# Layer 1 attention: the mask of each head moves from VectorE to GpSimd

## The chip, the cores and the metric

The kernel runs on one core of one Trainium2 chip. The metric is the device time of one launch in microseconds (us). The core has TensorE (PE) for matmuls, VectorE (DVE), ScalarE (ACT), GpSimd (POOL) and SyncE (SP), which issues the DMAs. Each engine works through its own instruction stream in order; between engines only semaphores order the work.

## The reference

Two transformer layers on 4 sequences of 1024 tokens with 128 channels. The change lies in the attention of layer 1, which keeps only the largest 30% of the scores of each row (`topk = 307` of 1024) and takes the softmax over those:

```python
topk = max(1, int(Tx * 0.3))
scores = jnp.einsum('bhid,bhjd->bhij', q, k) * scale
topk_scores, indices = jax.lax.top_k(scores, topk)
masked = jnp.full_like(scores, -jnp.inf)
masked = masked.at[bi, hi, ti, indices].set(topk_scores)
attn = jax.nn.softmax(masked, axis=-1)
out = jnp.einsum('bhij,bhjd->bhid', attn, v)
```

There are 16 heads and 32 blocks of 128 query rows, so 512 pairs of block and head, each with a score tile of 128 x 1024.

## The kernel before

`attention1` treats the 512 tiles ("heads" below) as a software pipeline written out by hand. Every engine runs the same frame, `tile_slots`: 16 slots for the first row block, a loop of 31 passes of 16 slots, and a tail. In slot h an engine does its own steps for heads h, h-1, h-2 and so on, by fixed lags. What a head goes through:

- TensorE, lag 0 (L1087): scores into the PSUM tile `S`. ScalarE (L1148) counts signs and makes a threshold `thr1` (L1159).
- VectorE, lag 1 (L1334): `z = S + thr1` into one of 8 ring buffers of `z`, with the row maximum. ScalarE (L1155) counts the signs of `z` and releases `cnt2`.
- GpSimd (its own slot h, after `cnt2` of head h): `shifted` (L1215), `side` (L1217), the large one `near` (L1221, 128 x 1024), and `rank` (L1224). In every fourth slot `split_max` (L1195 to L1205, five small steps for four heads) stands ahead of these, in another fourth slot `cut` and `gap` (L1229, L1232) stand behind them. `cut` is the exact threshold of each row for four heads.
- VectorE, lag 2: four MAX8 over quarters of `near` (L1363, L1373, L1379, L1391); lags 3 and 4: sorting the candidates, and `hits` (L1358), which finds the threshold `edge` and which reads two tiles in SBUF, `odd2` and `best`.
- VectorE, lag 8 (`PICK`): in every fourth slot the **check**: `flags` (L1325) from PSUM, and after `z` a load of its sum into a register (L1341) and a branch (L1342) that leads, for the rare rows with ties, into `general`, which rewrites `z` and `cut`. Then in every slot the **mask** (L1353): -2^40 where `z < cut`, into one of 4 buffers of `mask`.
- TensorE, lag 9: scores transposed plus mask, accumulated in `ST` (L1134, L1135); ScalarE takes the exponential (L1173); TensorE multiplies with v (L1103) four heads at a time.

In a VectorE slot the order is: (flags), wait for several semaphores, `z`, two small MAX8 (L1337, L1339), (register load, branch), wait `near_s` of head h-2, mask, `hits`, and the MAX8 mixed with the rest of the sort. The first wait for `near_s` stands ahead of the mask.

Of the kernel before, what the change touches and what calls it, by code (L numbers as in the profile page):

```python
# [930 lines left out]
def attention1(nc, k, search, ctx_all):  # L931
# [9 lines left out]
    with ExitStack() as ctx:  # L941
# [47 lines left out]
        mask_s, turned = sem("mask"), sem("turned")  # L989
# [193 lines left out]
        def _(pool):  # L1183
            CUTL = HIT - C2 - 1
# [22 lines left out]
            def slot(it, h):  # L1207
                n = lagged(it, h, 0, H, TOTAL)
                one = slice(h, h + 1)
                if n is not None:  # L1210
                    if h % 4 == 3:
                        pool.wait_ge(z_s, n + 1)
                        split_max(it, h)
# [10 lines left out]
                    pool.tensor_tensor(rank[:, one], sgn[1][:, one], shifted[:, one], ALU.mult).then_inc(rank_s, 1)  # L1224
                if lagged(it, h, CUTL, H, TOTAL) is not None and ends(h, CUTL):
                    l, h0 = nth(it, h, CUTL), (h - CUTL - 3) % H
                    four = slice(h0, h0 + 4)
                    pool.wait_ge(edge_s, l + 1)
                    pool.tensor_tensor(cut[:, four].bitcast(I32), side[:, four].bitcast(I32), edge[:, four].bitcast(I32),  # L1229
                                       ALU.subtract).then_inc(cut_s, 1)  # L1230

                    pool.tensor_tensor(gap[:, four], open_end[:, four], edge[:, four], ALU.subtract).then_inc(gap_s, 1)  # L1232
            tile_slots(pool, ITERS, H, CUTL + 1, slot)

        @block.vector
        def _(dve):
# [73 lines left out]
            def slot(it, h):  # L1310
# [38 lines left out]
                if picks:  # L1349
                    dve.wait_ge(cut_s, qp + 1)  # L1350
                    if not (isinstance(it, int) and lp < MASKS):
                        dve.wait_ge(turned, lp - (MASKS - 1))
                    dve.tensor_scalar(mask[:, hp % MASKS, :], z[:, hp % RING, :], cut[:, onep], AWAY,  # L1353
                                      ALU.is_lt, ALU.mult).then_inc(mask_s, 1)
# [662 lines left out]
```

## Time and profile before

| | us |
|---|---|
| median of 3 runs (4347.63 to 4366.65) | 4365.39 |
| the profiled execution | 4367.98 |
| its span, first to last instruction | 4366.2 |

| engine | busy us of the span | share |
|---|---|---|
| PE | 3242.5 | 74% |
| DVE | 3235.7 | 74% |
| ACT | 2490.3 | 57% |
| POOL | 1618.3 | 37% |

The page gives, for each engine, the busy time and the share of the span; then the span in 40 slices, where a digit is the busy share in tenths. The sparsified attention of layer 1 runs from about 1338 us to 3927 us. The timeline views give the start of each instruction and its duration in us, and in brackets how long its engine had sat idle before it and what released it. "issue" means that the engine waited for nothing that the profile shows. DVEq are instructions that VectorE's sequencer handles by itself (register loads, branches).

### The profile page before, as it was taken

Reading aid. Unit: us, or ns where it says so; the run is one execution under the profiler, and the core shown is the slowest. Engines: PE = TensorE matmul, PEld = TensorE weight load, DVE = VectorE, ACT = ScalarE, POOL = GpSimd, SP = SyncE. Lnnn points to the kernel's source line nnn. Section 1 sums busy time; section 2 is a strip of 40 time slices with the busy share of each in tenths; the row PEclk is TensorE's granted clock in tenths of the full one; section 3 lists DMA queues with packets and bytes.
Section 4 is the critical chain, followed back from the end, with each engine's and each line's share of the span. In section 5 each row is a group of like instructions: output and inputs, shape, how many; then the busy total and the mean of one; then the engine's idle time right before and its main releaser. Section 6 shows DMA issues by size and latency. Waiting matters only on the chain. (4 is left out here: it accounts for less than half of the span.)

```text
span 4366.2 us, 94950 instructions
## 1 busy us (share of the span) xinstructions
PE 3242.5 (74%) x25462; PEld 1877.8 (43%) x25510; DVE 3235.7 (74%) x12640; ACT 2490.3 (57%) x4604; POOL 1618.3 (37%) x3134
## 2 busy tenths in 40 slices
PE   3688888859375877766776776777775777775999
PEld 1233333446252444433443443444443444444565
DVE  6677777421647999977998996999987999994444
ACT  2255555523216777766776775777775777772222
POOL 3000000100024555544554554555554555553000
PEclk8699999969665555555555555555555555556999
DMA  3222222000012000001000001000001000000000
GB/s 104 36 37 28 33 30 32 2 14 24 22 60 35 6 5 4 6 9 25 4 6 4 4 10 27 4 6 4 4 12 25 4 6 4 5 2 25 5 7 7
DMA packets 130762, 74.95 MB, mean 17 GB/s; under 512 B 72791, under 2 KB 115559, under 8 KB 130455
## 3 DMA queue, kind: packets, MB, share of 16 engines
q1 hardware_dynamic: 130455, 72.22, 9.4%
q14 instruction: 281, 2.30, 0.2%
q8 instruction: 26, 0.43, 0.0%
HBM read 52.15 MB, written 19.14 MB: 16 GB/s over the span
## 5 line engine op out<-in xcount | busy, mean ns | idle before, releaser
L1134 PE MATMUL a_ST<-a_qs,a_ks 75*128 (+1 forms) x4096 | 880.6, 303 | 203.4 <-ACT a_eT L1173 145.5
L1221 POOL TENSOR_TENSOR a_near<-a_side,a_z 128x1024 int32<-128x1024 int32 x512 | 968.3, 1891 | 45.3 <-POOL a_side L1217 5.1
L1155 ACT ACTIVATE a_signs<-a_z,a_tiny 128x1024 bf16<-128x1024 f32 x512 | 588.1, 1149 | 608.4 <-DVE a_z L1334 608.4
L1135 PE MATMUL a_ST<-ident_b,a_mask 128*128 128x128 bf16 x4096 | 895.7, 306 | 0.0
L1334 DVE TENSOR_SCALAR_CACHE_REDUCE a_z<-a_S,a_thr 128x1024 f32<-128x1024 f32 x512 | 657.3, 1284 | 128.4 <-DVE a_cand L1391 60.4
L1134 PEld LDWEIGHTS a_ST<-a_qs,a_ks 75*128 75x128 bf16 x4096 | 570.6, 141 | 348.7 <-issue 341.3
L1087 PE MATMUL a_S<-a_ks,a_qs 72*128 72x512 bf16 x1024 | 505.3, 595 | 266.1 <-DVE a_z L1334 164.2
L1148 ACT ACTIVATE a_signs<-a_S,search 128x1024 bf16<-128x1024 f32 x512 | 564.0, 1102 | 75.0 <-PE a_S L1087 75.0
L1135 PEld LDWEIGHTS a_ST<-ident_b,a_mask 128*128 128x128 bf16 x4096 | 582.0, 142 | 0.1
L700 ACT ACTIVATE a_eT<-a_ST 128x512 f32<-128x512 f32 (+3 forms) x768 | 360.2, 490 | 378.8 <-PE a_ST L653 265.3
L1173 ACT ACTIVATE a_eT<-a_ST 128x1024 f32<-128x1024 f32 x512 | 512.8, 1002 | 34.4 <-PE a_ST L1135 34.3
L767 DVE TENSOR_REDUCE a_mx<-a_S 128x1 f32<-128x512 f32 (+3 forms) x768 | 388.8, 536 | 173.1 <-PE a_S L637 124.1
L1103 PE MATMUL a_O<-a_eT,a_v 128*9 128x128 f32 x8192 | 476.7, 392 | 26.7 <-DMA a_v<-v_ones 26.7
L1353 DVE TENSOR_SCALAR a_mask<-a_z,a_cut 128x1024 bf16<-128x1024 f32 x512 | 386.1, 754 | 50.6 <-DVE a_best L1339 9.6
L1103 PEld LDWEIGHTS a_O<-a_eT,a_v 128*9 128x9 f32 x8192 | 243.2, 118 | 375.0 <-issue 287.2
L637 PE MATMUL a_S<-a_ks,a_qs 72*128 (+4 forms) x768 | 274.4, 362 | 122.2 <-DMA a_ks<-k_parts 85.7
L1215 POOL TENSOR_TENSOR a_shifted<-a_sgn,a_miss 128x1 f32<-128x1 f32 x512 | 97.0, 189 | 592.7 <-ACT a_signs L1155 592.7
L718 POOL TENSOR_TENSOR ctxT<-a_num,a_rden 128x512 f32 (+1 forms) x32 | 40.6, 1269 | 616.6 <-DVE a_rden L799 616.6
L650 PE MATMUL a_ST<-a_qs,a_ks 128*128 (+4 forms) x720 | 240.4, 337 | 18.2 <-ACT a_eT L700 12.8
L1087 PEld LDWEIGHTS a_S<-a_ks,a_qs 72*128 (+1 forms) x1024 | 78.1, 116 | 369.2 <-issue 329.7
L1379 DVE MAX8 a_cand<-a_near 128x8 f32<-128x256 f32 x512 | 215.2, 420 | 0.0
L1363 DVE MAX8 a_cand<-a_near 128x8 f32<-128x256 f32 x512 | 214.1, 418 | 0.9 <-POOL a_near L1221 0.9
(327 smaller groups left out, 5641.5 us busy)
## 6 DMA issues: line engine op xcount, KB each, us to landing
a_ks<-k_parts SPq DMA_DIRECT2D x288, 64.0 KB
a_qs<-q_parts SPq DMA_DIRECT2D x144, 64.0 KB
a_qs<-q_parts SPq DMA_DIRECT2D x288, 32.0 KB
a_qs<-a_flip SPq DMA_DIRECT2D x512, 0.8 KB
q_parts<-p_qp SPq DMA_DIRECT2D x48, 128.0 KB, 1.7
k_parts<-p_kp SPq DMA_DIRECT2D x48, 128.0 KB, 1.8
f_w<-L_ffn_W SPq DMA_DIRECT2D x16, 256.0 KB, 2.6
v_ones<-p_vst SPq DMA_DIRECT2D x8, 288.0 KB, 2.4
```

The lines of the kernel that those rows point to most:

```text
L700: act.activation(eT[:, gi % 4, p % G, 0:hi - lo], ST[p % 2][:, 0:hi - lo], ACT.Exp, scale=SCALE0).then_inc(e_done, 1)
L767: dve.tensor_reduce(mx[:, lo // CW, j * IB + i:j * IB + i + 1], S[r % 3][:, 0:hi - lo], AX, ALU.max).then_inc(max_s, 1)
L1087: mm = pe.matmul(S[h % 2][:, lo:lo + CW], qa, ks[0:STACK, h * SEQ + lo:h * SEQ + lo + CW], start=True, stop=True)
L1103: mm = pe.matmul(O[32 * j:32 * j + HD + 1, :], v[:, kb, head], eT[:, h0 % RING + j, kb * P:(kb + 1) * P], start=(kb == 0), stop=(kb == IB ...
L1134: pe.matmul(ST[:, block_of], ks[:, hl * SEQ + kb * P:hl * SEQ + (kb + 1) * P], qa, start=True, stop=False)
L1135: mm = pe.matmul(ST[:, block_of], mask[:, hl % MASKS, block_of], k.ident_b[:, :], start=False, stop=True)
L1148: act.activation(signs[:, h % 2, :], S[h % 2][:, :], ACT.Sign, bias=first[:, bass.ds(n, 1)], accum_out=sgn[0][:, one]).then_inc(cnt1, 1)
L1155: act.activation(signs[:, 2, :], z[:, hl % RING, :], ACT.Sign, bias=tiny[:, :], accum_out=sgn[1][:, hl:hl + 1]).then_inc(cnt2, 1)
L1173: act.activation(eT[:, hl % RING, :], ST[:, :], ACT.Exp, scale=SCALE1).then_inc(e_done, 1)
L1221: pool.tensor_tensor(near[:, h % 2, :].bitcast(I32), side[:, one].bitcast(I32).broadcast_to([P, SEQ]), z[:, h % RING, :].bitcast(I32), ALU ...
L1334: dve.tensor_scalar(z[:, h1 % RING, :], S[h1 % 2][:, :], thr1[:, one1], None, ALU.add, ALU.max, accum_out=zmax[:, one1]).then_inc(z_s, 1)
L1353: dve.tensor_scalar(mask[:, hp % MASKS, :], z[:, hp % RING, :], cut[:, onep], AWAY, ALU.is_lt, ALU.mult).then_inc(mask_s, 1)
```

## The change

The mask of a head is no longer an instruction of VectorE but one of GpSimd, placed behind `near` and `rank` with a lag of 6 in GpSimd's own slots (`MASKL = PICK - C2 - 1`). VectorE tells with a new semaphore `check_s` when the check of four heads is done; GpSimd waits for it, and for a free mask buffer (`turned`), ahead of `shifted`, `side` and `near` of the same slot. `split_max` now stands ahead of that wait. VectorE gets a new wait ahead of `z`: the mask of the head that used this ring buffer before (`mask_s`). The tail of GpSimd's slots grows to 7.

```diff
             def slot(it, h):
                 n = lagged(it, h, 0, H, TOTAL)
                 one = slice(h, h + 1)
+                if n is not None and h % 4 == 3:
+                    pool.wait_ge(z_s, n + 1)
+                    split_max(it, h)
+                picks = lagged(it, h, MASKL, H, TOTAL) is not None
+                lp, hp = nth(it, h, MASKL), (h - MASKL) % H
+                if picks:
+                    pool.wait_ge(check_s, it * QD + (h - MASKL) // 4 + 1)
+                    if not (isinstance(it, int) and lp < MASKS):
+                        pool.wait_ge(turned, lp - (MASKS - 1))
                 if n is not None:
-                    if h % 4 == 3:
-                        pool.wait_ge(z_s, n + 1)
-                        split_max(it, h)
                     pool.wait_ge(cnt2, n + 1)
...
                     pool.wait_ge(shifted_s, n + 1)
                     pool.tensor_tensor(rank[:, one], sgn[1][:, one], shifted[:, one], ALU.mult).then_inc(rank_s, 1)
+                if picks:
+                    pool.tensor_scalar(mask[:, hp % MASKS, :], z[:, hp % RING, :], cut[:, hp:hp + 1], AWAY,
+                                       ALU.is_lt, ALU.mult).then_inc(mask_s, 1)
...
                 if has1 is not None:
+                    if not (isinstance(it, int) and l1 < RING):
+                        dve.wait_ge(mask_s, l1 - (RING - 1))
                     dve.wait_ge(thr1_s, l1 + 1)
...
                         with dve.Fori(0, 4) as j:
                             general(j, hp, qp)
+                    dve.nop().then_inc(check_s, 1)
...
-                if picks:
-                    dve.wait_ge(cut_s, qp + 1)
-                    if not (isinstance(it, int) and lp < MASKS):
-                        dve.wait_ge(turned, lp - (MASKS - 1))
-                    dve.tensor_scalar(mask[:, hp % MASKS, :], z[:, hp % RING, :], cut[:, onep], AWAY,
-                                      ALU.is_lt, ALU.mult).then_inc(mask_s, 1)
```

Where the instructions stand. GpSimd, at the turn from the fourth group's slot with `cut` to the next slot, before (the names are tiles, `a_shifted` is `shifted`; in brackets the semaphores waited for):

```order
L1224 TENSOR_TENSOR a_rank<-a_sgn,a_shifted 128x1 [waits a1_shifted]
L1229 TENSOR_TENSOR a_cut<-a_side,a_edge 128x4 [waits a1_edge]
L1232 TENSOR_TENSOR a_gap<-a_open_end,a_edge 128x4
L1215 TENSOR_TENSOR a_shifted<-a_sgn,a_miss 128x1 [waits a1_count2]
L1217 TENSOR_SCALAR a_side<-a_sgn 128x1
L1221 TENSOR_TENSOR a_near<-a_side,a_z 128x1024 [waits a1_top,a1_side]
L1224 TENSOR_TENSOR a_rank<-a_sgn,a_shifted 128x1 [waits a1_shifted]
L1195 TENSOR_TENSOR a_negmax<-a_thr,a_zmax 128x4 [waits a1_z]
```

The same place of GpSimd's stream in the changed kernel (its line numbers are 6 higher from `shifted` on):

```order
L1230 TENSOR_TENSOR a_rank<-a_sgn,a_shifted 128x1 [waits a1_shifted]
L1232 TENSOR_SCALAR a_mask<-a_z,a_cut 128x1024
L1238 TENSOR_TENSOR a_cut<-a_side,a_edge 128x4 [waits a1_edge]
L1241 TENSOR_TENSOR a_gap<-a_open_end,a_edge 128x4
L1221 TENSOR_TENSOR a_shifted<-a_sgn,a_miss 128x1 [waits a1_count2,a1_turned,a1_check]
L1223 TENSOR_SCALAR a_side<-a_sgn 128x1
L1227 TENSOR_TENSOR a_near<-a_side,a_z 128x1024 [waits a1_top,a1_side]
L1230 TENSOR_TENSOR a_rank<-a_sgn,a_shifted 128x1 [waits a1_shifted]
L1232 TENSOR_SCALAR a_mask<-a_z,a_cut 128x1024
L1195 TENSOR_TENSOR a_negmax<-a_thr,a_zmax 128x4 [waits a1_z]
```

A mask now stands in each slot, ahead of `cut` and ahead of `split_max` of the next slot, and `near` stands behind the wait for `check`.

VectorE, behind the branch of a check slot, before:

```order
L1352 REGISTER_ALU [waits a1_cut,a1_near,a1_sort]
L1353 TENSOR_SCALAR a_mask<-a_z,a_cut 128x1024 [waits a1_turned]
L1357 REGISTER_ALU [waits a1_rank]
L1358 SCALAR_TENSOR_TENSOR a_hits,a_edge<-a_odd,a_rank,a_best 128x24 [waits a1_sort]
L1361 MATCH_REPLACE a_rest<-a_best,a_cand 128x32
```

The same place in the changed kernel:

```order
L1363 REGISTER_ALU [waits a1_rank,a1_near,a1_sort]
L1364 SCALAR_TENSOR_TENSOR a_hits,a_edge<-a_odd,a_rank,a_best 128x24 [waits a1_sort]
L1367 MATCH_REPLACE a_rest<-a_best,a_cand 128x32
```

The mask is gone, and `hits` is the first instruction behind the wait for `near`.

## Rows read from the trace of the kernel before

**Rows 1.** The page: busy time and share by engine, and the 40 slices.
```profile
PE 3242.5 (74%) x25462; PEld 1877.8 (43%) x25510; DVE 3235.7 (74%) x12640; ACT 2490.3 (57%) x4604; POOL 1618.3 (37%) x3134
...
DVE  6677777421647999977998996999987999994444
```

**Rows 2.** Busy time by stretch: stage, one loop pass, one group of four slots.
```profile
core 0: us, PE busy (x) PEld busy (x) DVE busy (x) ACT busy (x) POOL busy (x), PEclk, DMA share, GB/s
2467.36:2545.47 78.11, 62.28 (x564) 37.43 (x564) 71.13 (x324) 58.55 (x108) 45.19 (x92) 0.52 0.03 5
...
2486.66:2505.75 19.09, 15.83 (x142) 9.40 (x143) 17.77 (x81) 14.64 (x28) 11.19 (x24) 0.50 0.00 1
1337.60:3926.80 2589.20, 1911.47 (x17729) 1153.88 (x17730) 2280.72 (x10355) 1863.76 (x3436) 1444.07 (x2940) 0.54 0.05 9
```

**Rows 3.** Timeline of VectorE: a check slot and the next `z`.
```profile
2505.75 1.28 DVE L1334 TENSOR_SCALAR_CACHE_REDUCE a_z<-a_S,a_thr 128x1024 f32<-128x1024 f32 x1 [0.26 <-DVE a_flags L1325]
...
2507.07 0.18 DVE L1339 MAX8 a_best<-a_cand 128x8 f32<-128x32 f32 x1
2507.28 0.75 DVE L1353 TENSOR_SCALAR a_mask<-a_z,a_cut 128x1024 bf16<-128x1024 f32 x1
2507.95 0.23 DVE L1358 SCALAR_TENSOR_TENSOR a_hits<-a_odd,a_rank,a_best 128x24 f32<-128x24 f32 x1
...
2510.39 1.28 DVE L1334 TENSOR_SCALAR_CACHE_REDUCE a_z<-a_S,a_thr 128x1024 f32<-128x1024 f32 x1 [0.24 <-DVE a_cand L1391]
```

**Rows 4.** VectorE's sequencer, 2440 to 2520 us: load of the flags' sum and branch.
```profile
L1342 DVEq COMPARE_BRANCH  x4: 56/70/72, 2447.1 to 2506.5; - x4
```

**Rows 5.** Timeline of GpSimd beside those slots.
```profile
2503.86 0.19 POOL L1215 TENSOR_TENSOR a_shifted<-a_sgn,a_miss 128x1 f32<-128x1 f32 x1
...
2504.31 1.89 POOL L1221 TENSOR_TENSOR a_near<-a_side,a_z 128x1024 int32<-128x1024 int32 x1
2506.16 0.19 POOL L1224 TENSOR_TENSOR a_rank<-a_sgn,a_shifted 128x1 f32<-128x1 f32 x1
2507.12 0.20 POOL L1195 TENSOR_TENSOR a_negmax<-a_thr,a_zmax 128x4 f32<-128x4 f32 x1 [0.77 <-DVE a_z L1334]
2507.40 0.68 POOL L67 TENSOR_TENSOR a_parts<-a_negmax,ones 128x4 bf16<-128x4 f32 x1
2508.16 0.20 POOL L1201 TENSOR_TENSOR a_left<-a_negmax,a_parts 128x4 f32<-128x4 f32 x1
2508.44 0.20 POOL L67 TENSOR_TENSOR a_parts<-a_left,ones 128x4 bf16<-128x4 f32 x1
```

**Rows 6.** Timelines of VectorE and GpSimd: `z` of a head, then its `shifted`.
```profile
2477.06 1.28 DVE L1334 TENSOR_SCALAR_CACHE_REDUCE a_z<-a_S,a_thr 128x1024 f32<-128x1024 f32 x1 [0.24 <-DVE a_cand L1391]
```
```profile
2479.71 0.19 POOL L1215 TENSOR_TENSOR a_shifted<-a_sgn,a_miss 128x1 f32<-128x1 f32 x1 [2.25 <-ACT a_signs L1155]
```

**Rows 7.** Groups of instructions by line: candidates for the mask's price on GpSimd.
```profile
L1353 DVE TENSOR_SCALAR a_mask<-a_z,a_cut 128x1024 bf16<-128x1024 f32 x512 | 386.1, 754 | 50.6 <-DVE a_best L1339 9.6 <-issue 6.4 <-DVE a_flags L1325 1.0
```
```profile
L1221 POOL TENSOR_TENSOR a_near<-a_side,a_z 128x1024 int32<-128x1024 int32 x512 | 968.3, 1891 | 45.3 <-POOL a_side L1217 5.1
...
L713 POOL COPY a_vx<-a_vst 128x128 f32 x28 | 8.2, 291 | 37.0 <-PE a_O L667 37.0
L882 POOL COPY o_c_in<-ctx 128x512 f32 x8 | 4.9, 612 | 19.8 <-PEq L889 19.0 <-PE o_cT_ps L897 0.8
```

**Rows 8.** Durations in ns (min/median/max): a VectorE op with two SBUF inputs; two of GpSimd.
```profile
L324 DVE TENSOR_TENSOR p_qres<-p_qf,p_qp x16: 674/681/1611, 47.1 to 1292.7; 128x512 f32<-128x512 f32 x16
```
```profile
L1358 DVE SCALAR_TENSOR_TENSOR a_hits<-a_odd,a_rank,a_best x512: 226/238/243, 1346.1 to 3933.0; 128x24 f32<-128x24 f32 x171
```
```profile
L67 POOL TENSOR_TENSOR a_parts<-a_negmax,ones x128: 198/202/690, 1346.3 to 3923.0; 128x4 bf16<-128x4 f32 x128
```

**Rows 9.** Timelines of both engines near 48 us: L328 has two SBUF inputs.
```profile
48.25 1.52 DVE L328 TENSOR_TENSOR p_qp<-p_qres,p_qp 128x512 bf16<-128x512 f32 x1
```
```profile
48.03 1.20 POOL L409 TENSOR_TENSOR p_kres<-p_kf,p_kp 128x512 f32<-128x512 f32 x1 [43.41 <-ACT p_kp L395]
```

**Rows 10.** Timelines at the loop's top: VectorE, and GpSimd's `shifted` and `near`.
```profile
2466.96 0.15 DVE L1325 TENSOR_SCALAR_CACHE_REDUCE a_flags<-a_OT 1x4 f32<-1x4 f32 x1 [2.07 <-issue]
```
```profile
2474.89 0.19 POOL L1215 TENSOR_TENSOR a_shifted<-a_sgn,a_miss 128x1 f32<-128x1 f32 x1 [1.96 <-ACT a_signs L1155]
...
2475.42 1.89 POOL L1221 TENSOR_TENSOR a_near<-a_side,a_z 128x1024 int32<-128x1024 int32 x1 [0.16 <-POOL a_side L1217]
```

More of the change, by code:

```diff
@@ L988, in attention1 @@
         flag_p, flag_v, gap_s = sem("flag_p"), sem("flag_v"), sem("gap")
-        mask_s, turned = sem("mask"), sem("turned")
+        mask_s, turned, check_s = sem("mask"), sem("turned"), sem("check")
         pv, oc, ot, rd, normed = sem("pv"), sem("o_copied"), sem("o_turned"), sem("rden"), sem("normed")
@@ L1183, in _ @@
         def _(pool):
-            CUTL = HIT - C2 - 1
+            CUTL, MASKL = HIT - C2 - 1, PICK - C2 - 1
             pool.memset(miss2[:, :], 2 * MISS).then_inc(pool_const, 1)
@@ L1232, in slot @@
                     pool.tensor_tensor(gap[:, four], open_end[:, four], edge[:, four], ALU.subtract).then_inc(gap_s, 1)
-            tile_slots(pool, ITERS, H, CUTL + 1, slot)
+            tile_slots(pool, ITERS, H, MASKL + 1, slot)
         @block.vector
```

## The prediction

> **What bounds the kernel now.** I read the page first: PE and DVE are both busy 74% of the span, but DVE's slices stand at 9 and above through most of the layer 1 attention [rows 1]. The busy time by stretch says what that stage is worth: 2589 us, and in a clean group of four slots DVE is busy 17.8 of 19.09 us, ACT 14.6, PE 15.8 and POOL 11.2 [rows 2]. So DVE's order of work sets the slot. Then the timelines. One loop pass of 16 heads takes 78.11 us [rows 2], of which 2.07 us are a stall of DVE at the loop's top [rows 10]; (78.11 - 2.07) / 4 = 19.0 us for a **group** of four slots. There are 128 groups.
>
> POOL looks half idle, but it isn't free at any time. It can begin `near` of a head only after that head's `z` on DVE and the sign count on ACT, and DVE wants `near` in its very next slot. The reader is to see in [rows 5] that `near` ends at 2506.20 and in [rows 3] that DVE passes its wait for it ahead of 2507.28: only 1.1 us of slack in each slot.
>
> **What is removed.** The mask on DVE: 754 ns [rows 7], start to start 0.67 us (2507.28 to 2507.95, [rows 3]), four per group: -2.68 us. If nothing else moved: 512 x 0.67 = 343 us. Also, `split_max` on POOL was stretched where it met the mask (0.68 against 0.20 us, [rows 5]); it now takes 4 x 0.28 + 0.15 = 1.27 us.
>
> **What is added on POOL: the mask's price M.** No row has a tensor-scalar of this size on POOL. From below: COPY, also one tensor input, 612 ns for 512 columns and 291 for 128 [rows 7], so 0.84 ns a column and 1.04 us for 1024. From above: `near`, two inputs, 1.89 us. It is nearer to COPY by its inputs, but it compares, multiplies and converts: I take M = 1.3.
> The Trainium skill (GPSIMD Engine Reference, Performance versus the Vector engine) gives 1.03 cycles an element at 1.2 GHz for bodies of at most two operations and 2.03 for comparisons that aren't unrolled: an estimate of 0.9 or 1.7 us, by which the sum below would be +0.1 or +1.3 us a group. Its advice (Engine selection) is to keep elementwise work on VectorE; the rows agree in so far as even COPY's rate is slower than the 0.75 us that DVE needs.
>
> **What is added as a wait.** `check_s` is raised by DVE in the check slot, and POOL waits for it ahead of `shifted`, `side`, `near` of the head whose `near` DVE wants in that same slot. Before, this `near` ran during the slot ahead. Queued behind the wait on POOL are `near`, `rank`, the mask, and the next slot's `split_max`; DVE waits for the first. How early is the check? The branch runs at 2506.5 [rows 4], 0.7 to 0.8 us after `z` began at 2505.75, so the sequencer runs ahead of DVE's own work; I put `check_s` at 0.85.
>
> **The group, step by step** (0 is the start of `z` in the check slot A; slots B, C, D follow). Constants: without the mask DVE is ready for `hits` 1.53 us after `z` starts (2505.75 to 2507.28); `hits` to the next `z` is 2.44 in A (2507.95 to 2510.39) [rows 3], which makes A 4.64 long; the other three slots share the remaining 14.36 of 19.0, 4.79 each, so 4.79 - 1.53 - 0.67 = 2.6 from `hits` to the next `z`. `shifted` to `near` 0.45, `near` 1.89 [rows 5]. `shifted` can't start before 2.65 after its head's `z` (2477.06 to 2479.71, [rows 6]), which puts `near`'s end 5.0 after `z`.
> - A: POOL starts at 0.9, `near` ends 3.25, DVE's `hits` 3.3 instead of 1.53: **1.75 us of stall**. Mask 3.35 to 4.65.
> - B: `z` 5.75, ready 7.3. POOL: `split_max` 1.27, `shifted`/`side` 0.45, `near` to 8.25. `hits` 8.3: **1.0 of stall**. Mask 8.35 to 9.65.
> - C: `z` 10.9, ready 12.45. `near` 10.1 to 12.0, mask 12.1 to 13.4.
> - D: `near` ends at 5.0 after C's `z`, 15.9; mask 16.0 to 17.3.
>
> In C and D `near` is in time, but DVE meets the mask itself. `hits` reads two SBUF tiles. The rows show such an instruction held while POOL works: L324 takes 674 or 1611 ns, never more in between than POOL's work explains, and L328 at 48.25 takes 1.52 us beside a POOL instruction that ends at 49.23 [rows 8, 9]; the other way round, `a_parts` is stretched to 690 by DVE's mask [rows 8]. So I let `hits` wait for the mask's end: C 13.4 instead of 12.45, **0.95 of stall**; D's `z` 16.0, ready 17.55, behind the mask's end, no stall; the next A's `z` at 17.55 + 2.6 = 20.15.
> The Trainium skill (SBUF — State Buffer, Who interferes with whom) states it as a lock: a VectorE instruction with two SBUF inputs and a GpSimd instruction that reads SBUF exclude each other for the whole instruction. L328's row agrees; for `hits`, never above 243 ns in 512 [rows 8], the trace before can't tell, since no long POOL instruction ran beside it.
>
> Sum: 20.15 - 19.0 = +1.15 us a group, x 128 = **+147 us**. The same steps with M = 1.04 give 19.4 (+0.4, 51 us), with M = 1.89 give 21.0 (+2.0, 256 us; there `near` is late in every slot, and `cut`, `gap` behind the last mask make the flags late).
>
> **The loop's top.** DVE stalls 2.07 us there for nothing shown; POOL sat idle 1.96 us at its own top and was still 0.16 late for `near` [rows 10]. So a reload of up to about 2 us is hidden under POOL's idle time now. Behind the change POOL has no idle time there (C follows a mask). Bounds 0 and 2.07 us x 31 = 64; I take 1 us: **+31**.
>
> **Hidden.** The new wait on `mask_s` ahead of `z` asks for a mask made 3 slots before its `z`: free up to M of 2.3 us. PE gets a mask up to 1.5 us later in the group; its transposed matmuls also wait for the exponential, which comes 2.6 us after `z` and later than the mask: 0. ACT is busy 14.6 of 19 [rows 2]: 0. The wait on `turned` is met by a slot: 0. `check_s` itself is a sequencer's step: 0.
>
> Forecast: span 4366.2 + 147 + 31 = 4544; the profiled run lies 1.8 us above its span and 2.6 above the median: **4543 us**.
>
> **Rivals.**
> 1. *`hits` loses the race* (0.2). When `near` ends, POOL goes on to `rank` and the mask 0.1 us later, and DVE's `hits`, released by the same event, comes while `rank` reads. If the mask gets in first, `hits` waits M more in A, and in B to the end of that mask. With M = 1.3: `hits` stands at 4.65, 9.65, 13.8 and 18.65, the next `z` at 21.25: +2.25 a group, with the loop's top 4366 + 288 + 31 = 4685. For: POOL's instructions start back to back [rows 5]. Against: DVE asks first.
> 2. *M near 1.9* (0.2): 4366 + 256 + 31 = 4653.
> 3. *M near COPY's* (0.2): 4366 + 51 + 31 = 4448, or 4417 without the loop term.
> 4. *No contention for `hits`* (0.1), if tiles of 24 columns don't hold DVE. Then only the stalls of A and B are left, 1.75 and M - 0.3, against 2.68 of masks: M = 1.3 gives `hits` at 3.3, 8.3, 12.45, 16.6 and `z` at 19.2 (+0.2, 26 us), M = 1.04 gives 18.95 (-0.05). With the loop's top between 4360 and 4423: mostly no change. **Faster** is this case with a cheap mask: it decides where M falls below 1.1; at VectorE's own 0.75 us the group is 18.65, -0.35, -45 us, 4321 without the loop term.
> 5. *The move acts as meant* (0.02): if `near` weren't behind the check, -343 us, 4023. The order rows speak against it.
>
> **How the numbers follow.** My own case has 0.28. The range holds it, rival 3, most of rivals 1 and 2 and the upper part of 4: 4385 to 4730; left out are M and a lost race together above, and a cheap mask below. Anything within 0.5% (22 us) is about what a measurement of this kernel can't tell from no change. Faster by more: 0.06 (rival 5 and the cheap end of 4). Within: 0.10 (most of the rest of 4, the low end of 3). Slower: 0.84.
>
> **What would show it.** In the changed profile: (a) the mask on POOL with its mean duration; (b) DVE idle ahead of `hits`, released by POOL's `near`, once or twice a group, some 1.8 and 1.0 us, in all above 300 us; (c) `hits` with a maximum far above 243 ns, or late by the mask's length, if contention is real; (d) POOL's busy time up by 512 x M; (e) a group of about 20.2 us and DVE's busy time down by 386 us; (f) an idle time of POOL at the loop's top. Wrong would be: `near` released ahead of the check, or M above 2.3, where the ring wait ahead of `z` bites.

## The result, and the profile after

The changed kernel takes **5494.01 us** in the median of 4 runs (5481.41 to 5500.54) against 4363.31 us (4347.63 to 4366.65) of the kernel before: ratio **1.2605**, 95% interval 1.2575 to 1.2634. It is slower, as forecast, but by 1131 us where 178 were forecast (4543, range 4385 to 4730).

The page of the changed kernel: busy time by engine, and the slices of VectorE and GpSimd. They answer to [rows 1].

```profile
PE 3262.7 (59%) x25510; PEld 1914.4 (35%) x25510; DVE 3304.4 (60%) x12128; ACT 2505.3 (46%) x4604; POOL 3461.2 (63%) x3646
...
DVE  5877762164666666666666666666666666664444
...
POOL 2000001013888987889798888889888988898200
```

GpSimd's busy time more than doubled (1618 to 3461 us), and in the attention stage its slices now stand at 8 and 9 where VectorE's have fallen to 6. The bound moved from VectorE to GpSimd. The stage by the busy times of a stretch, beside [rows 2]:

```profile
core 0: us, PE busy (x) PEld busy (x) DVE busy (x) ACT busy (x) POOL busy (x), PEclk, DMA share, GB/s
1357.90:5072.60 3714.70, 1925.82 (x17910) 1197.93 (x17910) 2337.05 (x9790) 1865.88 (x3408) 3265.58 (x3422) 0.53 0.03 5
```

GpSimd is busy 3266 of 3715 us. TensorE's granted clock is 0.53 in this stage, as before (0.54), so the clock isn't the cause. The groups of instructions by line say which instruction it is (columns: busy us, mean ns of one | idle time of the engine just before, with what ended it); the first two answer to [rows 7], the third to [rows 8]:

```profile
L1232 POOL TENSOR_SCALAR a_mask<-a_z,a_cut 128x1024 bf16<-128x1024 f32 x512 | 1908.4, 3728 | 2.0 <-DVEq L1356 2.0
L1227 POOL TENSOR_TENSOR a_near<-a_side,a_z 128x1024 int32<-128x1024 int32 x512 | 968.9, 1892 | 45.0 <-POOL a_side L1223 5.1
...
L1345 DVE TENSOR_SCALAR_CACHE_REDUCE a_z<-a_S,a_thr 128x1024 f32<-128x1024 f32 x512 | 657.4, 1284 | 355.5 <-POOL a_mask L1232 309.7 <-DVE a_flags L1334 30.9 <-ACT a_thr L1159 14.3
...
L1364 DVE SCALAR_TENSOR_TENSOR a_hits<-a_odd,a_rank,a_best 128x24 f32<-128x24 f32 x512 | 523.0, 1021 | 779.7 <-issue 324.9 <-DVE a_best L1350 202.2 <-POOL a_rank L1230 169.6
```

One mask costs GpSimd **3.73 us**, five times VectorE's 0.75 and twice `near`, which the prediction took for the upper bound. The timeline of GpSimd over a group (start us, duration; in brackets how long it was idle, and what released it), beside [rows 5]:

```profile
3002.23 3.73 POOL L1232 TENSOR_SCALAR a_mask<-a_z,a_cut 128x1024 bf16<-128x1024 f32 x1
3005.92 0.20 POOL L1238 TENSOR_TENSOR a_cut<-a_side,a_edge 128x4 int32<-128x4 int32 x1
3006.07 0.20 POOL L1241 TENSOR_TENSOR a_gap<-a_open_end,a_edge 128x4 f32<-128x4 f32 x1
3008.76 0.19 POOL L1221 TENSOR_TENSOR a_shifted<-a_sgn,a_miss 128x1 f32<-128x1 f32 x1 [2.48 <-DVEq L1356]
3008.91 0.23 POOL L1223 TENSOR_SCALAR a_side<-a_sgn 128x1 f32<-128x1 f32 x1
3009.22 1.89 POOL L1227 TENSOR_TENSOR a_near<-a_side,a_z 128x1024 int32<-128x1024 int32 x1
3011.07 0.19 POOL L1230 TENSOR_TENSOR a_rank<-a_sgn,a_shifted 128x1 f32<-128x1 f32 x1
3011.24 3.73 POOL L1232 TENSOR_SCALAR a_mask<-a_z,a_cut 128x1024 bf16<-128x1024 f32 x1
3014.93 0.20 POOL L1195 TENSOR_TENSOR a_negmax<-a_thr,a_zmax 128x4 f32<-128x4 f32 x1
...
3016.20 0.19 POOL L1221 TENSOR_TENSOR a_shifted<-a_sgn,a_miss 128x1 f32<-128x1 f32 x1
...
3022.38 0.19 POOL L1221 TENSOR_TENSOR a_shifted<-a_sgn,a_miss 128x1 f32<-128x1 f32 x1
```

A slot of GpSimd is 6.18 us (3016.20 to 3022.38) with nothing idle in it. A group is 4 x 6.18 = 24.7, plus 1.27 of `split_max` (3014.93 to 3016.20), 0.3 of `cut` and `gap`, and 2.48 idle at the wait for the check: 28.8 us. VectorE's `z` in the check slots stands 28.81 us apart (3007.21 and 3036.02), where it was 19.0 before. The stage has 29.0 us for each group (3714.7 / 128), so nearly all of it is this one chain. The same group on VectorE, beside [rows 3]:

```profile
3006.85 0.15 DVE L1334 TENSOR_SCALAR_CACHE_REDUCE a_flags<-a_OT 1x4 f32<-1x4 f32 x1 [1.50 <-PE a_OT L1113]
...
3007.21 1.28 DVE L1345 TENSOR_SCALAR_CACHE_REDUCE a_z<-a_S,a_thr 128x1024 f32<-128x1024 f32 x1 [0.21 <-DVE a_flags L1334]
...
3011.30 1.09 DVE L1364 SCALAR_TENSOR_TENSOR a_hits<-a_odd,a_rank,a_best 128x24 f32<-128x24 f32 x1 [2.60 <-POOL a_rank L1230]
...
3015.19 1.28 DVE L1345 TENSOR_SCALAR_CACHE_REDUCE a_z<-a_S,a_thr 128x1024 f32<-128x1024 f32 x1 [0.83 <-POOL a_mask L1232]
...
3018.74 1.10 DVE L1364 SCALAR_TENSOR_TENSOR a_hits<-a_odd,a_rank,a_best 128x24 f32<-128x24 f32 x1 [2.06 <-issue]
```

VectorE waits in each slot: ahead of `flags` (which need `gap`, and `gap` stands behind the fourth mask on GpSimd), ahead of `hits`, and ahead of `z` for a ring buffer that the mask still reads. And `hits`, 0.24 us of work, takes 1.1: it starts 0.06 us behind the mask.

### The profile page after: what moved, and what is told of

It reads as the page before. It is cut to its first block and busy times, and to the rows that moved or that the text cites. A ratio compares the mean times of both kernels' runs of the same rounds, so it can differ in the third digit from the quotient of the medians.

```text
span 5498.8 us, 95725 instructions
## 1 busy us (share of the span) xinstructions
PE 3262.7 (59%) x25510; PEld 1914.4 (35%) x25510; DVE 3304.4 (60%) x12128; ACT 2505.3 (46%) x4604; POOL 3461.2 (63%) x3646
## 5 line engine op out<-in xcount | busy, mean ns | idle before, releaser
L1232 POOL TENSOR_SCALAR a_mask<-a_z,a_cut 128x1024 bf16<-128x1024 f32 x512 | 1908.4, 3728 | 2.0 <-DVEq L1356 2.0
L1364 DVE SCALAR_TENSOR_TENSOR a_hits<-a_odd,a_rank,a_best 128x24 f32<-128x24 f32 x512 | 523.0, 1021 | 779.7 <-issue 324.9
L1345 DVE TENSOR_SCALAR_CACHE_REDUCE a_z<-a_S,a_thr 128x1024 f32<-128x1024 f32 x512 | 657.4, 1284 | 355.5 <-POOL a_mask L1232 309.7
L1087 PE MATMUL a_S<-a_ks,a_qs 72*128 72x512 bf16 x1024 | 538.7, 629 | 102.7 <-DMA a_ks<-k_parts 55.3
L1103 PE MATMUL a_O<-a_eT,a_v 128*9 128x128 f32 x8192 | 502.4, 409 | 32.7 <-DMA a_v<-v_ones 32.7
L409 POOL TENSOR_TENSOR p_kres<-p_kf,p_kp 128x512 f32<-128x512 f32 x16 | 21.6, 1350 | 399.9 <-ACT p_kp L395 399.9
L650 PE MATMUL a_ST<-a_qs,a_ks 128*128 (+4 forms) x768 | 259.9, 342 | 18.7 <-ACT a_eT L700 12.9
L1112 PE MATMUL a_OT<-a_twice,ones 128*1 128x4 f32 x256 | 24.8, 167 | 340.4 <-ACT a_hidden L1167 340.2
```

Source lines behind the costliest of these rows:

```text
L1087: mm = pe.matmul(S[h % 2][:, lo:lo + CW], qa, ks[0:STACK, h * SEQ + lo:h * SEQ + lo + CW], start=True, stop=True)
L1103: mm = pe.matmul(O[32 * j:32 * j + HD + 1, :], v[:, kb, head], eT[:, h0 % RING + j, kb * P:(kb + 1) * P], start=(kb == 0), stop=(kb == IB ...
L1232: pool.tensor_scalar(mask[:, hp % MASKS, :], z[:, hp % RING, :], cut[:, hp:hp + 1], AWAY, ALU.is_lt, ALU.mult).then_inc(mask_s, 1)
L1364: dve.scalar_tensor_tensor(hits[:, :], odd2[:, :], rank[:, one4], best[:, h4 % 2, :], ALU.is_equal, ALU.mult, accum_out=edge[:, one4]).the ...
```

## The experiments

First theory: the time is two costs that hardly overlap, the price of the mask on GpSimd and the wait for the check ahead of `near`. Rivals: the mask is slow only because VectorE is in its way; the wait costs nothing beside such a mask; a hold between the two engines makes the most of it.

**The price by itself.** The kernel before, with a tail on GpSimd behind its attention of layer 1: twelve forms of instruction, three times each, with no other work on GpSimd. Four of the first list:

```diff
+                pool.tensor_scalar(pb[:, :], px[:, :], pc[:, 0:1], AWAY, ALU.is_lt, ALU.mult).then_inc(price_s, 1)
...
+                pool.tensor_scalar(py[:, :], px[:, :], pc[:, 0:1], None, ALU.is_lt).then_inc(price_s, 1)
...
+                pool.tensor_scalar(py[:, :], px[:, :], 0.5, 2.0, ALU.mult, ALU.add).then_inc(price_s, 1)
...
+                pool.tensor_copy(py[:, :], px[:, :]).then_inc(price_s, 1)
```

> Price list: the kernel before, with a tail on GpSimd behind its slots of the layer 1 attention in which each of 12 forms of a 128 x 1024 instruction runs alone, three times, each behind the end of the one ahead. The mask's form (f32 in, a threshold for each row, is_lt then mult, bf16 out) took 3.73 us in the changed kernel. Theory 'form': it is the price of the two-step tensor-scalar itself, so it costs 3.7 us here too, with VectorE idle, 1.9 us at 512 columns, and about half with one step (is_lt alone). Rival 'contention': 3.73 us holds waits for VectorE, and alone it costs 1.0 to 1.9 us. Second rival 'output type': f32 out is clearly cheaper than bf16 out. COPY of 1024 columns should be 1.04 us by the two COPY rows of before.

One instruction's durations in ns (min/median/max) with their starts; L1241 is the mask's own form, L1245 the same into f32, L1249 the comparison alone, L1253 a multiplication alone, L1255 multiply and add, L1263 a copy:

```profile
L1241 POOL TENSOR_SCALAR a_pb<-a_px,a_pc x3: 3714/3714/4619, 3930.4 to 3990.3; 128x1024 bf16<-128x1024 f32 x3
L1245 POOL TENSOR_SCALAR a_py<-a_px,a_pc x3: 3703/3704/3704, 3937.3 to 3996.2; 128x1024 f32<-128x1024 f32 x3
L1249 POOL TENSOR_SCALAR a_py<-a_px,a_pc x3: 2843/2843/2844, 3944.0 to 4002.9; 128x1024 f32<-128x1024 f32 x3
L1253 POOL TENSOR_SCALAR a_py<-a_px x3: 2782/2782/2782, 3950.7 to 4009.6; 128x1024 f32<-128x1024 f32 x3
L1255 POOL TENSOR_SCALAR a_py<-a_px x3: 1047/1047/1048, 3953.5 to 4012.4; 128x1024 f32<-128x1024 f32 x3
L1263 POOL COPY a_py<-a_px x3: 1037/1042/1042, 3959.7 to 4018.6; 128x1024 f32<-128x1024 f32 x3
```

3.71 us in a quiet place: the price is the form's own, not VectorE's doing and not the conversion's (3.70 into f32). The 4.62 us is the first of the three; it ran beside the last four masks of VectorE. One step alone was expected at about half and takes three quarters (2.84). The copy at 1.04 us is what [rows 7] were read to give, but it says nothing about a comparison. A second list asked which forms are cheap.

> Second price list, as the first, with 12 other forms on GpSimd (128 x 1024 unless said). In the first list a tensor-scalar with two immediate steps mult, add took 1.05 us, one step is_lt 2.85, is_lt and mult 3.7, mult alone 2.78, and a tensor-tensor mult 1.89. Theory 'a fast path': only mult then add (perhaps also add or mult with a value for each row) is fast, about 1.05 us, and everything else costs 2.8 us for one step and 3.7 for two. Rival 'comparisons are slow': add, min and mult forms of any kind are at 1.0 to 1.9 us and only is_lt costs more. At 256 columns the mask's form should take 1.1 us (2.00 at 512 and 3.71 at 1024 make 3.35 ns a column and 0.28 us fixed).

```profile
L1243 POOL TENSOR_SCALAR a_py<-a_px,a_pc x3: 1117/1117/1423, 3925.6 to 3976.1; 128x1024 f32<-128x1024 f32 x3
L1245 POOL TENSOR_SCALAR a_py<-a_px,a_pc x3: 2850/2852/3196, 3927.1 to 3977.3; 128x1024 f32<-128x1024 f32 x3
L1253 POOL TENSOR_SCALAR a_py<-a_px x3: 3639/3639/3639, 3935.5 to 3985.4; 128x1024 f32<-128x1024 f32 x3
L1255 POOL TENSOR_SCALAR a_pb<-a_px,a_pc x3: 1189/1189/1189, 3939.3 to 3989.1; 128x1024 bf16<-128x1024 f32 x3
```

Add then multiply is 1.12 us (L1243), the add alone 2.85 (L1245), minimum then multiply 3.64 (L1253), multiply then add with two column operands 1.19 (L1255). One step is dearer than two: only the pairs of add and multiply that were tried are quick.

**The wait alone.** The mask stays on VectorE; only `check_s` is added, ahead of `shifted`:

```diff
+                    if lagged(it, h, PICK - C2 - 1, H, TOTAL) is not None:
+                        pool.wait_ge(check_s, it * QD + (h - (PICK - C2 - 1)) // 4 + 1)
                     pool.wait_ge(cnt2, n + 1)
...
+                    dve.nop().then_inc(check_s, 1)
```

> The kernel before, mask still on VectorE, with only the new wait: GpSimd waits for the check of four heads ahead of shifted, side and near. Theory 'price of the mask': the wait costs what step A of the prediction said, near ends 3.25 us after z of the check slot, VectorE ready at 1.53: +1.75 us a group, 224 us, about 4590 us; less if near stands nearer. Rival 'the wait is the cause': most of the +1130 us, above 5000 us. Rival 'hidden': no change.

Measured 4637.1 us, +274, ratio 1.0617 (1.0552 to 1.0683). A check slot, VectorE and then GpSimd:

```profile
3018.40 1.28 DVE L1336 TENSOR_SCALAR_CACHE_REDUCE a_z<-a_S,a_thr 128x1024 f32<-128x1024 f32 x1 [0.26 <-DVE a_flags L1327]
...
3021.97 0.75 DVE L1356 TENSOR_SCALAR a_mask<-a_z,a_cut 128x1024 bf16<-128x1024 f32 x1 [2.08 <-issue]
```
```profile
3019.54 0.19 POOL L1217 TENSOR_TENSOR a_shifted<-a_sgn,a_miss 128x1 f32<-128x1 f32 x1 [2.97 <-DVEq L1347]
...
3019.99 1.89 POOL L1223 TENSOR_TENSOR a_near<-a_side,a_z 128x1024 int32<-128x1024 int32 x1
```

VectorE comes to its next instruction 3.57 us after `z` began instead of 1.53 [rows 3]: 2.04 us a group, x 128 = 261 of the 274. GpSimd starts 1.14 us after `z` here; the prediction had 0.9.

**The mask alone.** The change with its two waits, for the check and for a free mask buffer, moved behind `near`:

```diff
-                if picks:
-                    pool.wait_ge(check_s, it * QD + (h - MASKL) // 4 + 1)
...
                 if n is not None:
                     pool.wait_ge(cnt2, n + 1)
...
+                if picks:
+                    pool.wait_ge(check_s, it * QD + (h - MASKL) // 4 + 1)
...
+                if n is not None:
                     pool.wait_ge(shifted_s, n + 1)
                     pool.tensor_tensor(rank[:, one], sgn[1][:, one], shifted[:, one], ALU.mult).then_inc(rank_s, 1)
```

> The changed kernel with the waits for the check and for a free mask buffer moved behind near, ahead of rank. The mask stays on GpSimd. Theory 'price': GpSimd is then never idle for long; its own work is 4 x (0.45 + 1.89 + 0.15 + 3.7) + 1.3 + 0.3 = 26.4 us a group against the 28.8 measured in the trace of the changed kernel: about -2.4 x 128 = -300 us, 5190 us. Rival 'the wait is the cause': back to within 250 us of before, 4400 to 4600 us.

Measured 5199.65 us, +836, ratio 1.1905 (1.1832 to 1.1978). GpSimd runs without a gap but for 1.6 us at the loop's top; a group is 26.46 us, 2.35 less than with the wait ahead. The two parts add up: 274 + 836 = 1110 of the 1131 us.

**A smaller price.** Both of the change's parts, but the mask covers only the first columns, 320 and 512 of 1024; the rest of `mask` stays zero, so part of the scores isn't masked.

```diff
-                    pool.tensor_scalar(mask[:, hp % MASKS, :], z[:, hp % RING, :], cut[:, hp:hp + 1], AWAY,
+                    pool.tensor_scalar(mask[:, hp % MASKS, 0:320], z[:, hp % RING, 0:320], cut[:, hp:hp + 1], AWAY,
                                        ALU.is_lt, ALU.mult).then_inc(mask_s, 1)
```

> The changed kernel, its mask made for the first 320 of 1024 columns alone (the rest of the mask stays zero, so the softmax runs over more scores than it should). If the price goes with the columns, the mask takes about 1.3 us, the value that the prediction took. Theory 'only M was wrong': the group is then 20.15 us by the prediction's steps and the time about 4543 us (4500 to 4600). Rival 'the steps are wrong too': outside 4450 to 4650 us.

> The changed kernel with the mask made for 512 of 1024 columns (the rest stays zero). Mask 2.0 us. By the prediction's steps the value for 1.89 us was 21.0 us a group, 4653 us; for 2.0 us about 21.5 a group, 4720 us. For hits, which lasted 1.10 us beside a mask of 1024 columns and 0.51 beside one of 320: theory 'it is held while GpSimd reads its input, 0.83 ns a column': 0.24 + 0.43 = 0.67 us. Rival 'it is held for the whole instruction': above 1.5 us.

Measured: 320 columns, mask 1.38 us, 4545.9 us, ratio 1.0408 (1.0348 to 1.0469); 512 columns, mask 2.02 us, 4724.1 us, ratio 1.0852 (1.0802 to 1.0902). With nearly the price that the prediction assumed (1.3), the time is nearly the one predicted (4543). Slots B and C of the first show that this is partly luck. GpSimd's masks of B and C, then VectorE's `hits` of B and C:

```profile
3014.70 1.38 POOL L1233 TENSOR_SCALAR a_mask<-a_z,a_cut 128x320 bf16<-128x320 f32 x1
...
3018.52 1.38 POOL L1233 TENSOR_SCALAR a_mask<-a_z,a_cut 128x320 bf16<-128x320 f32 x1
```
```profile
3014.75 0.51 DVE L1365 SCALAR_TENSOR_TENSOR a_hits<-a_odd,a_rank,a_best 128x24 f32<-128x24 f32 x1 [0.80 <-DVE a_best L1351]
...
3019.25 0.24 DVE L1365 SCALAR_TENSOR_TENSOR a_hits<-a_odd,a_rank,a_best 128x24 f32<-128x24 f32 x1
```

In B `hits` starts 0.05 us behind the mask and is held to 0.51; in C it starts in the middle of a mask that runs to 3019.90 and isn't held. So C's stall of 0.95 us doesn't exist, while A was worse than said: its `hits` began at 4.06 us after `z`, not 3.3, and was held 0.3 more, as it was in B. These errors nearly cancel: a group is 20.39 us where 20.15 was said. A held `hits` takes 0.51 us beside 320 columns (the row above), up to 0.67 beside 512 and 1.10 beside 1024: 0.24 us and 0.83 to 0.84 ns for each column of the mask, not the 3.35 ns a column that the mask's own duration has. The hold has a fixed end: in the changed kernel a `hits` that started 0.34 us into the mask instead of 0.05 took 0.81 us instead of 1.10, and both end 1.15 us after the mask's start.

**Both parts made small.** 320 columns (again part of the scores isn't masked) and the wait behind `near`.

> The changed kernel with both: the mask for 320 of 1024 columns (1.38 us, the rest zero) and the waits for check and mask buffer behind near instead of ahead of it. Theory 'two causes, each enough': with neither of them GpSimd's own work is 4 x (0.45 + 1.89 + 0.15 + 1.38) + 1.6 = 17.1 us a group, VectorE's is 16.3, so the group is 17.1 to 18.3 us against 19.0 before: faster, 4120 to 4280 us. Rival 'contention eats it': hits held twice or more a group, 19 us or above, 4360 us or more.

Measured 4230.83 us, ratio 0.9719 (0.9668 to 0.977). With a short mask and the wait out of the way, giving VectorE's mask away does gain. The question is then whether a complete kernel can get there.

**Sharing.** The kernel before, but GpSimd makes 448 columns of the masks of two heads in four, VectorE the rest; waits behind `near`.

```diff
+                if picks:
+                    pool.tensor_scalar(mask[:, hp % MASKS, 0:LEAD], z[:, hp % RING, 0:LEAD], cut[:, hp:hp + 1], AWAY,
+                                       ALU.is_lt, ALU.mult).then_inc(part_m, 1)
...
-                    dve.tensor_scalar(mask[:, hp % MASKS, :], z[:, hp % RING, :], cut[:, onep], AWAY,
+                    lo = LEAD if hp % 4 in SHARE else 0
+                    dve.tensor_scalar(mask[:, hp % MASKS, lo:], z[:, hp % RING, lo:], cut[:, onep], AWAY,
```

> An attempt at a better kernel, complete: the kernel before, in which GpSimd makes the first 448 of 1024 columns of the masks of the third and fourth head of each four (1.78 us each, in its idle time behind near) and VectorE the other 576 and the first two heads whole. VectorE saves 448 x 0.65 ns = 0.29 us twice a group, at most 128 x 0.58 = 75 us: 4290 us. Rival 'the shared port': VectorE's mask is held while GpSimd's part runs, or GpSimd's part while VectorE's runs, and near comes later: 4360 us or more.

Measured 4396.63 us, ratio 1.01 (1.0069 to 1.0131). A pair of the two parts, VectorE's and GpSimd's:

```profile
3010.89 0.79 DVE L1373 TENSOR_SCALAR a_mask<-a_z,a_cut 128x576 bf16<-128x576 f32 x1
```
```profile
3009.55 1.81 POOL L1238 TENSOR_SCALAR a_mask<-a_z,a_cut 128x448 bf16<-128x448 f32 x1
```

VectorE's 576 columns take 0.50 us at the shortest, but 0.67 in the mean of 256. When they started 1.25 to 1.5 us into GpSimd's part, as above, they took 0.62 to 0.87 us. When they started 0.97 to 1.16 us into it (98 of 256), they took 0.52, and GpSimd's part was stretched from 1.81 to 1.9 or 2.1. So VectorE saves 256 x (0.755 - 0.674) = 21 us of the 75 hoped for, and the kernel is 43 us slower; where those are lost wasn't looked for.

**Another form of the mask.** GpSimd computes the difference, VectorE turns its sign into the mask in place (bf16):

```diff
+                    pool.tensor_scalar(mask[:, hp % MASKS, :], z[:, hp % RING, :], cut[:, hp:hp + 1], 2.0 ** 60,
+                                       ALU.subtract, ALU.mult).then_inc(diff_s, 1)
...
+                if picks:
+                    dve.wait_ge(diff_s, lp + 1)
+                    dve.tensor_scalar(mask[:, hp % MASKS, :], mask[:, hp % MASKS, :], 0.0, AWAY, ALU.is_lt, ALU.mult).then_inc(mask_s, 1)
                 if has2 is not None:
                     dve.max(found[:, 24:32], quarter(3)).then_inc(top_s, 1)
```

> A complete kernel. GpSimd keeps the subtraction, VectorE keeps the comparison. The wait for the check stands behind `near` (as in e2_wait_behind). GpSimd writes (z - cut) * 2^60 into the mask's bf16 buffer: a two-step subtract-and-multiply, of the kind that the price runs show at 1.12 us instead of 3.73. VectorE turns it into the mask in place (is it below 0, times -1e30; bf16 in and out, no wait in the hot spot ahead of `hits`), just ahead of its last MAX8. The wait ahead of `z` for a free buffer goes by GpSimd's pass. My theory (two causes: the price of the form, and the wait that stands ahead of `near`; with both gone VectorE's work sets the group again): GpSimd per group 4 x (2.49 + 1.12) + 1.57 = 16.0 us, below VectorE's 16.3 + 4 x 0.35 = 17.7; a group of about 17.9 to 18.6 and a time of 4240 to 4330 us, faster than before. Rival (contention: `hits` is held while GpSimd reads, up to 0.85 us in two slots of four, and the small work behind the pass comes late): no gain, 4360 us or more.

> A complete kernel. The same two passes as f6_diff, but the wait for the check stands where the change put it, ahead of `shifted` and `near`. It is the change at the price of the mask that the prediction assumed (1.1 against 1.3 us), over all 1024 columns. With 320 columns and a mask of 1.38 us a group took 20.39 us; here GpSimd's pass is 0.26 shorter, VectorE has 0.35 more in each of four slots: between 20.1 (its added work falls into slots where it waited anyhow) and 21.8: 4460 to 4680 us, most likely 4580, slower than before. Rival (the wait matters only beside a long mask): about the time of f6_diff.

Both miss their ranges: 5496.17 us, ratio 1.2622 (1.2594 to 1.2649), and, with the wait ahead of `near`, 5788.02 us, 1.3283 (1.3246 to 1.3321). Subtract-and-multiply isn't one of the quick pairs:

```profile
L1233 POOL TENSOR_SCALAR a_mask<-a_z,a_cut 128x1024 bf16<-128x1024 f32 x512 | 1926.5, 3763 | 52.7 <-DVEq L1357 1.7
...
L1399 DVE TENSOR_SCALAR a_mask<-a_mask 128x1024 bf16<-128x1024 bf16 x512 | 218.6, 427 | 960.6 <-POOL a_mask L1233 960.6
```

I had inferred the price of `subtract` from that of `add` (1.12 us); it is 3.76. The price isn't all: with the same price and the same place of the wait e2_wait_behind took 5200 us. The other 297 us came with VectorE's second pass and its wait for GpSimd's (960.6 us in all); no run separates the two. So the next pair takes the measured form itself, z times -1 plus `cut`, and asks whether that is above 0:

```diff
-                    pool.tensor_scalar(mask[:, hp % MASKS, :], z[:, hp % RING, :], cut[:, hp:hp + 1], 2.0 ** 60,
-                                       ALU.subtract, ALU.mult).then_inc(diff_s, 1)
+                    pool.tensor_scalar(mask[:, hp % MASKS, :], z[:, hp % RING, :], less1[:, :], cut[:, hp:hp + 1],
+                                       ALU.mult, ALU.add).then_inc(diff_s, 1)
```

> A complete kernel: f6_diff with another form of the same pass. In f6_diff GpSimd's subtract-and-multiply took 3.76 us, the slow price. Here GpSimd computes cut - z as z times -1 (a column) plus cut (a column), the form that the second price run shows at 1.19 us, and VectorE asks whether that is above 0 (0.43 us, as measured in f6_diff). The wait stands behind `near`. By the rows of f6_diff GpSimd's four slots would take (7.96 - 3.77 + 1.19) + 2 x (6.69 - 3.77 + 1.19) + (6.98 - 3.77 + 1.19) = 18.0 us, VectorE's work is 16.3 + 4 x 0.43 = 18.0: both near the 19.0 of before. My theory (the price of the form is what cost f6_diff and the change their time): 1150 us or so below f6_diff, a group of 18.2 to 19.2 us, 4270 to 4400 us. Rival (VectorE's wait for GpSimd's pass, 960 us in f6_diff, is a matter of order and stays in part even with a short pass): above 4450 us.

> A complete kernel: f9_negdiff with the wait for the check where the change put it, ahead of `shifted` and `near`. It is the change with a short GpSimd pass (1.19 us; the prediction assumed 1.3) over all columns. The wait alone cost 2.1 us a group in e1_wait_alone. Theory (the wait costs that much whatever the mask): f9_negdiff + 128 x 2.1 = 270 us, between 4500 and 4680. Rival (the wait hides behind VectorE's wait for the pass): within 80 us of f9_negdiff.

The pass on GpSimd took 1.20 us as expected, but the kernel 4768.52 us, ratio 1.0939 (1.0917 to 1.0962). That is 728 us less than with the slow form, but neither the 4270 to 4400 of the theory nor the rival's reason: VectorE's wait for the pass has gone (5.0 us in all). A third cause is in the rows of VectorE's own pass over the mask; the line of durations, then VectorE and GpSimd in three slots:

```profile
L1399 DVE TENSOR_SCALAR a_mask<-a_mask x512: 396/1779/1946, 1360.7 to 4348.8; 128x1024 bf16<-128x1024 bf16 x171
```
```profile
3002.87 0.83 DVE L1365 SCALAR_TENSOR_TENSOR a_hits<-a_odd,a_rank,a_best 128x24 f32<-128x24 f32 x1
...
3005.26 0.40 DVE L1399 TENSOR_SCALAR a_mask<-a_mask 128x1024 bf16<-128x1024 bf16 x1
...
3015.72 1.78 DVE L1399 TENSOR_SCALAR a_mask<-a_mask 128x1024 bf16<-128x1024 bf16 x1
```
```profile
3002.47 1.20 POOL L1233 TENSOR_SCALAR a_mask<-a_z,a_less,a_cut 128x1024 bf16<-128x1024 f32 x1
...
3005.34 2.07 POOL L1223 TENSOR_TENSOR a_near<-a_side,a_z 128x1024 int32<-128x1024 int32 x1
...
3015.33 1.89 POOL L1223 TENSOR_TENSOR a_near<-a_side,a_z 128x1024 int32<-128x1024 int32 x1
```

Started 0.39 us behind `near`, VectorE's pass takes 1.78 us and ends 0.3 us after it (3017.50 against 3017.22); started 0.08 us ahead, it takes 0.40, and `near` is the one stretched, to 2.07. The mean is 1.37 instead of 0.43: 512 x 0.94 = 480 us of VectorE. `hits` is held too: started 0.40 us into GpSimd's pass, it takes 0.83 us and ends 0.03 us after it. With the wait put back ahead of `near` (f10_negdiff_wait) it is 4911.82 us, ratio 1.1272 (1.1243 to 1.1301), +143 where I had +270 or under 80. The pass meets `near` less often there (mean 1.10 us, 134 us less in sum) and `hits` is held less (57 us less), which pays for part of the wait.

Was it the hold? The same kernel with VectorE's pass moved up to between GpSimd's pass and the next `near`:

```diff
                     dve.match_replace(rest[0][:, :], ranked[:, 0:8], mine, GONE).then_inc(sort_s, 1)
+                if picks:
+                    dve.wait_ge(diff_s, lp + 1)
+                    dve.tensor_scalar(mask[:, hp % MASKS, :], mask[:, hp % MASKS, :], 0.0, AWAY, ALU.is_gt, ALU.mult).then_inc(mask_s, 1)
...
-                if picks:
-                    dve.wait_ge(diff_s, lp + 1)
-                    dve.tensor_scalar(mask[:, hp % MASKS, :], mask[:, hp % MASKS, :], 0.0, AWAY, ALU.is_gt, ALU.mult).then_inc(mask_s, 1)
```

> A complete kernel: f9_negdiff with VectorE's pass over the mask moved up, from behind the third MAX8 (where its trace shows it beside GpSimd's `near`, 1.78 us in the median instead of 0.43) to right behind `hits`' MATCH_REPLACE8, which by that trace lies between the end of GpSimd's pass and the start of the next `near`. Theory (a bf16 pass of VectorE and `near` keep each other out of SBUF, and that, 512 x (1.37 - 0.43) = 480 us, is why f9_negdiff is slower than before): the pass takes 0.4 to 0.6 us in the mean, VectorE waits for GpSimd's pass up to 0.6 us a slot instead; a group of 18.5 to 20 us, 4300 to 4480 us. Rival (the pass is slow for another reason, in place for instance, or `near` catches it here too): mean above 1.2 us and a time within 80 us of f9_negdiff's 4769.

```profile
L1371 DVE TENSOR_SCALAR a_mask<-a_mask x512: 408/416/478, 1357.2 to 3988.8; 128x1024 bf16<-128x1024 bf16 x171
...
L1365 DVE SCALAR_TENSOR_TENSOR a_hits<-a_odd,a_rank,a_best x512: 242/244/850, 1340.4 to 3980.4; 128x24 f32<-128x24 f32 x171
```

4423.19 us, 345 less by the place of one instruction, ratio 1.0146 (1.0129 to 1.0163) to the kernel before. The hold was the third cause. The move took 486 us from VectorE's pass (699 to 213 us in all); `hits` (34 us more) and new waits take part of that back. What is left over the kernel before is small change: 0.42 us of pass in each slot, `hits` held in some slots (mean 0.42 instead of 0.24), 62 us of waiting for GpSimd's pass. No complete kernel of these beats the one before.

## Why the prediction was wrong

- **The price M: the step that failed.** "It is nearer to COPY by its inputs [...] I take M = 1.3", between 1.04 and 1.89. The mask measured 3.73 us in place and 3.71 alone. Neither bound was one: no row of the trace before had a compare-and-multiply of any large size on GpSimd, and the number of inputs, by which I placed it, isn't what sets the price there. With a bound that doesn't exclude anything the range should have been open above. The Trainium skill (GPSIMD Engine Reference) has 1.03 cycles an element in the section Performance versus the Vector engine, and 2.03 for a comparison that isn't unrolled in the section Performance pitfalls for Q7 kernels; at its 1.2 GHz that is an estimate of 0.9 or 1.7 us. The measured 3.73 us is over twice the dearer one, so the trace disagrees. Only the add-and-multiply pairs, at 1.04 to 1.19 us, come near its cheap figure.
- **M above 2.3 and the ring wait.** The text named this as what would make it wrong, and it happened: VectorE waits 309.7 us ahead of `z` for GpSimd's mask. In those slots GpSimd has no idle time, so the wait is the form in which its pace reaches VectorE rather than a cost of its own.
- **"DVE's order of work sets the slot".** True before; behind the change GpSimd's 26.3 us of work a group (4 x 6.18 and 1.6) are above VectorE's 19.0 - 2.68 = 16.3. I added M to a chain of events slot by slot and never held GpSimd's sum against the group. With M = 1.3 that sum was harmless: the same slots would be 26.3 - 4 x 2.43 = 16.6 us.
- **The wait ahead of `near`.** Right in kind: slot A stalls, and e1_wait_alone has 2.04 us a group for it. The start of GpSimd in A was 0.9 in the prediction, 1.14 with the mask on VectorE and 1.55 in the changed kernel (3007.21 to 3008.76).
- **Who waits for whom at the check.** I priced the wait from VectorE's side only. It also closes a circle: `flags` need `gap`, `gap` stands behind the fourth mask on GpSimd, and GpSimd then waits for the check of those flags with nothing to do, 2.48 us a group, x 128 = 317 us. e2_wait_behind gives back 5494 - 5200 = 294.
- **The race of rival 1.** It was given 0.2, and `hits` does lose it: 0.24 us became 1.10 in the median. But the price is 0.84 ns a column, not M. That is COPY's rate in [rows 7], so it may be the time in which GpSimd reads its input; no run shows that. "I let `hits` wait for the mask's end", in slots C and D, was wrong for this form: in e3_w320 it ran in the middle of a mask at 0.24 us. Beside the quick form of f9_negdiff it would have been right. The Trainium skill (SBUF — State Buffer, Who interferes with whom) has the exclusion for the whole instruction; `near` against the bf16 pass agrees (1.78 us, to its end), and so does the 1.20-us pass against a `hits` started 0.40 us into it; the mask of 3.73 us against `hits` doesn't: held 0.86 us, or not at all.
- **The loop's top.** +31 us was wrong in sign. Before, the group with the loop's top takes 20.7 us between `flags` and `flags`, 1.6 more than the others. In the changed kernel eight in a row are all 28.66 to 28.81: the stall at the top hides in VectorE's waits, which gives 31 x 1.6 = 50 us back. With the short mask of e3_w320 that group is 21.9 us, again about 1.6 more than its neighbours, so there the term was 0. About 50 us more come back in three stretches of five groups, where the sequence changes: 23 to 29 us each before, 29 to 36 after. That is why 128 x 9.8 = 1254 us is more than the 1131 measured; over all groups the mean went from 20.3 to 29.2 us.
- **PE, ACT, `turned`: 0.** Right. TensorE waits 1126 us for masks, but only ScalarE's exponential waits for it in turn, 46 us, and no wait for `turned` shows.

By its own signs: (a) was there and out of bounds, (b) there (2.60 and 2.06 us ahead of `hits`), (c) there, (d) there in kind, up by 1843 us where 666 were meant, (e) false (28.8, and VectorE's busy time not down by 386 but up by 69; `hits` alone is 402 longer), (f) absent.

## What to carry to other kernels

Before work moves to another engine, the exact instruction (operations, operands, width) has to be timed there; a neighbour with as many inputs, or `add` for `subtract`, gives no bound, and where it can't be timed the range stays open above. Then hold the new sum of the receiving engine against the period before any slot is stepped through. And a sync point put ahead of an engine's most urgent instruction costs by itself: here 274 us with no work moved at all, and in the changed kernel moving it three instructions back gave 294 back. Beside a short GpSimd pass it cost less (143 us in f10_negdiff_wait).

## What the runs showed of the hardware

- GpSimd's tensor-scalar over 128 x 1024: comparison and multiply 3.70 to 3.73 us with the threshold in a column, 3.63 with a constant one; `subtract` and multiply 3.76, minimum and multiply 3.64; one step alone 2.77 to 2.85, whatever it is of those tried; multiply and add, in either order, 1.04 to 1.19. Two steps can cost little more than a third of one.
- Whether `hits` is held beside the slow form is decided by about 0.1 us: 0.06 us behind the mask's start it takes 1.10 us, and in f6_diff 0.07 us ahead of it (3012.67 against 3012.74) 0.24. Beside the quick form of f9_negdiff it is another moment: 0.05 us behind the start `hits` takes 0.24 us, 0.37 to 0.41 us behind it 0.82 to 0.85.
- A bf16 pass of VectorE over 1024 columns, 0.40 to 0.43 us by itself, takes up to 1.95 us beside `near` in f9_negdiff and 2.04 in f10_negdiff_wait. Before the change VectorE's mask began 1.1 us behind `near`'s end [rows 3, 5] and took 737 to 778 ns in all 512 cases, so nothing there showed this. Whether an f32 mask would be held as long beside `near` wasn't tried; beside GpSimd's own masks f32 masks of VectorE were held, or held the other: in p1_prices one that started 0.49 us into GpSimd's mask took 1.61 us instead of 0.75, and that mask 4.62 instead of 3.71 (see also f4_share448).
